# Attention and mixture layers in one pipelined kernel: other order and other buffers in the first and in the last iterations

## What is computed

```python
x = x + attn_a(layernorm(x))     # 16 heads of 8 channels, rotary, causal
x = x + ffn(layernorm(x))
x = x + attn_b(layernorm(x))     # the same form, other weights and angles
x = x + ffn(layernorm(x))

def ffn(x):                      # 8 heads of 64 channels, 5 experts, 2 picked
    wv = topk_mask(x @ Ws, 2) * sigmoid(x @ Ws)          # per token and head
    v = einsum('bthe,btek->bhtk', wv, einsum('btd,edk->btek', x, Wv))
    probs = softmax(einsum('bhid,bhjd->bhij', q * scale, k))
    attn = einsum('bhij,bhjd->bihd', probs, v)
    return einsum('bthe,bthk,ekd->btd', topk_mask(x @ Wd, 2), attn, Wo)
```

## Time and profile before

| | value |
|---|---|
| median of 3 runs | 1955.2 us |
| the profiled execution's own time | 1959.13 us |
| its span, first to last instruction | 1957.4 us |
| PE busy | 1787.4 us (91%) |
| DVE busy | 1570.6 us (80%) |
| ACT busy | 1274.1 us (65%) |
| POOL busy | 1049.5 us (54%) |
| mean granted TensorE clock | 0.977 |
| PE in the 40 slices of the span | 4878999999999999999999999999999999998894 |

### The profile page before, as it was taken

How to read it: one execution, slowest core, us unless ns; L and a number is a source line. 1 busy time by engine, 2 the same in 40 slices (tenths; PEclk the granted TensorE clock), 3 DMA queues, 4 the chain that set the end, 5 groups by cost and what they waited for, 6 DMA issues and landing times.

```text
span 1957.4 us, 32660 instructions
## 1 busy us (share of the span) xinstructions
PE 1787.4 (91%) x11328; PEld 894.7 (46%) x11328; DVE 1570.6 (80%) x2936; ACT 1274.1 (65%) x2803; POOL 1049.5 (54%) x1124
## 2 busy tenths in 40 slices
PE   4878999999999999999999999999999999998894
PEld 2343545445454544545455454544545454453443
DVE  6487888889888798988879788887978888797661
ACT  1547577675857768586775857667585766758461
POOL 1416374665637466463746646374664647555533
PEclk8989999999999999999999999999999999999887
DMA  2211011110101111110111111011110101100000
GB/s 78 62 43 33 12 39 39 45 39 31 47 12 40 38 45 39 31 44 15 39 39 45 38 31 36 22 39 39 44 40 31 31 28 39 39 11 21 1 11 6
DMA packets 87361, 66.61 MB, mean 34 GB/s; under 512 B 10592, under 2 KB 82976, under 8 KB 87200
## 3 DMA queue, kind: packets, MB, share of 16 engines
q1 hardware_dynamic: 87200, 64.52, 10.8%
HBM read 30.42 MB, written 8.39 MB: 20 GB/s over the span
## 4 chain that ended last, share of the span: by engine, by line
PE 54%; DVE 30%; ACT 10%; issue 3%; POOL 1%; DMA 1%; SPq 0%; POOLq 0%; PEld 0%; DVEq 0%; PEldq 0%; ACTq 0%
PE Y L494 9%; DVE nmaxA L877 7%; DVE ztmp L992 6%; PE S1c L433 5%; PE S2a L459 4%; PE S1b L433 4%; DVE nmaxF L882 4%; ACT Pq L721 4%; PE S2b L459 4%; PE Y L485 4%; PE M L587 3%; PE M L545 3%; ACT PT L706 3%; DVE ztmp L964 2%; PE M L599 2%
## 5 line engine op out<-in xcount | busy, mean ns | idle before, releaser
L1110 POOL TENSOR_TENSOR Z<-Z,ztmp 128x1280 f32<-128x1280 f32 x112 | 324.6, 2898 | 339.9 <-DVE ztmp L992 338.8
L1077 POOL TENSOR_SCALAR_AFFINE_SELECT PT<-PT 128x256 f32<-128x256 f32 (+1 forms) x640 | 256.3, 410 | 290.9 <-ACT PT L706 285.8
L1101 POOL TENSOR_TENSOR Vf<-Vf,ztmp 128x512 f32<-128x512 f32 x256 | 349.0, 1363 | 94.4 <-DVE ztmp L964 85.8
L706 ACT ACTIVATE PT<-S2a 128x512 f32<-128x512 f32 x320 | 191.8, 599 | 132.5 <-PE S2a L453 126.1
L494 PE MATMUL Y<-PT,Vf 128*64 128x512 f32 x1024 | 267.8, 614 | 0.0
L710 ACT ACTIVATE PT<-S2a 128x512 f32<-128x512 f32 x256 | 153.4, 599 | 151.5 <-PE S2a L459 148.1
L964 DVE TENSOR_TENSOR ztmp<-xv,wv_s 128x512 f32<-128x512 f32 x256 | 240.2, 938 | 2.8 <-POOL Z L1110 2.8
L433 PE MATMUL S1c<-Kf,Qf 64*128 64x512 f32 x352 | 201.8, 654 | 26.8 <-ACT Pq L721 25.7
L433 PE MATMUL S1a<-Kf,Qf 64*128 64x512 f32 x352 | 201.4, 652 | 25.6 <-ACT Pq L721 25.6
L706 ACT ACTIVATE PT<-S2b 128x512 f32<-128x512 f32 x320 | 191.9, 600 | 25.9 <-PE S2b L453 25.6
L433 PE MATMUL S1b<-Kf,Qf 64*128 64x512 f32 x320 | 183.3, 653 | 10.2 <-ACT Pq L721 10.1
(11 more groups left out here) (111 smaller groups left out, 3729.8 us busy)
## 6 DMA issues: line engine op xcount, KB each, us to landing
Qs<-parts SPq DMA_DIRECT2D x96, 128.0 KB
Ks<-parts SPq DMA_DIRECT2D x96, 128.0 KB
tab_s<-in_tab SPq DMA_DIRECT2D x16, 512.0 KB, 4.4
out_x<-res SPq DMA_DIRECT2D x32, 256.0 KB, 2.2
xr<-out_x SPq DMA_DIRECT2D x24, 256.0 KB, 2.9
wa_s<-in_wa SPq DMA_DIRECT2D x16, 320.0 KB, 3.2
xl<-in_x SPq DMA_DIRECT2D x8, 256.0 KB, 3.0
Qs<-mrowA SPq DMA_DIRECT2D x128, 4.0 KB, 1.7
```

The costliest lines, as they stand in the source:

```text
L706: nc.scalar.activation(PT[:, slot % 2, b, :], t[:, :], ACT.Exp, scale=SCALE_A).then_inc(exps_done.sem, 1)
L1101: nc.gpsimd.tensor_tensor(Vf[:, i, :, :], Vf[:, i, :, :], vtmp[:, n % VBUF, :, :], ALU.add).then_inc(v_acc.sem, 1)
L1110: nc.gpsimd.tensor_tensor(Z[:, :, :, :], Z[:, :, :, :], ztmp[:, hh % 2, :, :, :], ALU.add).then_inc(z_acc.sem, 1)
```

## The change

It touches iterations 0, 17 and 18; the code of the others is as before.

- Iteration 0: the keys are rotated in `first_keys`, memory of `Pq` that has no use yet, so their rotation waits no longer for the queries' third part. The 6 scatters of the keys are issued by ACT. All 98 rows of `Ks` are set to ones in one memset of 4-byte words; the memset of two rows is gone. PE steps over absent uses with fewer waits.
- Iteration 17: the order of uses is `LAST_USES`, with "F q2" and "F k2" ahead of "YT7", and their projection is at (0, 6), not (1, 6). The product of the last head (hh = 7) is at (2, 5), not (1, 3). The buffers of the value products lie in `PT`, and the second value product waits no longer for the last sum into Z. Uses that have no work are all stepped over at the iteration's start.
- Iteration 18: heads 4 and 5 are multiplied as before, but POOL adds only tokens 256 to 511 (the second half of the four 128-token tiles), and DVE the first half. Heads 6 and 7 are multiplied and added by DVE alone, half by half. Transposes, copies, the product with `wo_s`, the residual and the store come in two halves, in the banks S1a to S1c, S2a and S2b.

```diff
...
+    TWO_ONES = float(np.array([0x3F803F80], np.uint32).view(np.float32)[0])
...
+        first_keys = Pq[:, 0, 0:2, :]
...
+        LAST_USES = ["YT6", "F q2", "F k2", "YT7", "F q3", "F k3", "ZT0", "ZT1", "ZT2", "F out", "YT4", "YT5"]
...
-                late = [u for u in uses if u in ("ZT0", "ZT1", "ZT2", "F out")]
-                uses = [u for u in uses if u not in late]
-                first = uses.index("A yNT" if "A yNT" in uses else "YT2")
-                uses = uses[:first] + late + uses[first:]
+                uses = [u for u in uses if u not in LAST_USES] + [u for u in LAST_USES if u in uses]
...
+        def f_steps(k):
+            return F_STEPS[:2] + [(0, 6)] + F_STEPS[3:] if k == UNITS + 1 else F_STEPS
+        def mix_step(k, g, h):
+            return (2, 5) if (k, g, h) == (UNITS + 1, 3, 1) else ((SA + g + 2) % NS, 2 * h + 1)
+        def vtmp_of(k, n):
+            return PT[:, n % VBUF // 2, NF_B + n % 2, :].rearrange("p (h d) -> p h d", h=HF) if k == UNITS + 1 else vtmp[:, n % VBUF, :, :]
...
+        def turning(j, qk):
+            return (first_keys[:, 0, :], first_keys[:, 1, :]) if j == 0 and qk else (rot, rot2)
...
-                if f_end:
+                if f_end and j < LAST - 1:
                     sp.wait_ge(resF_ready.sem, resF_ready.at(j, 1, 3))
                     sp.dma_start(stream(j - 3), res[:, :, :]).then_inc(resF_stored.sem, 16)
+                if j == LAST - 1:
+                    for half in range(2):
+                        sp.wait_ge(tail_ready, half + 1)
+                        sp.dma_start(stream(j - 3)[:, HALVES[half], :], res[:, HALVES[half], :]).then_inc(tail_stored, 16)
...
+                        if j == 0 and qk:
+                            continue
...
+                    if j == UNITS + 1 and use not in LAST_USES and not at_start:
+                        return
+                    if j or place(j, use) > place(j, "A xnT" if use in M0_USES else "A q"):
+                        pe.wait_ge(*free_for(j, use))
                     pe.sem_inc(is_full(use), 1)
                     pe.sem_inc(is_free(use), 1)
...
+                def last_output():
+                    for half in range(2):
+                        pe.wait_ge(tail_sums, half + 1)
+                        for c, (lo, hi) in enumerate(ZCH):
+                            for i in range(NT)[HALVES[half]]:
+                                zi = Z_wide[:, i, :, :].rearrange("p e d -> p (e d)")
+                                last = nc.tensor.transpose(S1[c][0:hi - lo, i * P:(i + 1) * P], zi[:, lo:hi], ident[:, :])
+                            last.then_inc(tail_ZT_filled, 1)
+                        pe.wait_ge(tail_ZT_drained, len(ZCH) * (half + 1))
+                        for i in range(NT)[HALVES[half]]:
+                            for c, (lo, hi) in enumerate(ZCH):
+                                last = nc.tensor.matmul(S2[half][:, i * C:(i + 1) * C], ZT[0:hi - lo, c, i * P:(i + 1) * P],
+                                                        wo_s[0:hi - lo, c, :], start=(c == 0), stop=(c == 2))
+                        last.then_inc(tail_out_filled, 1)
...
+                at_start = True
+                if j == UNITS + 1:
+                    for use in M0_USES + M1_USES:
+                        if use not in LAST_USES:
+                            skip(use)
+                at_start = False
...
+                        if j == LAST - 1 and at == (1, 0):
+                            last_output()
...
-                        if at in F_STEPS:
-                            f_project(F_STEPS.index(at))
+                        if at in f_steps(j):
+                            f_project(f_steps(j).index(at))
...
+                        if j == 0 and at == (4, 4):
+                            act.wait_ge(rows_zeroed.sem, rows_zeroed.per)
+                            act.wait_ge(part2_ready.sem, part2_ready.at(j, 2))
+                            for r in range(NSP):
+                                act.dma_start(Ks[rows_of(r), :, :],
+                                              parts[:, 1, SPLITS_K[r], :]).then_inc(scattered.sem, 16)
...
+                        if j == LAST - 1 and at == (1, 1):
+                            for half in range(2):
+                                for c, (lo, hi) in enumerate(ZCH):
+                                    act.wait_ge(tail_ZT_filled, len(ZCH) * half + c + 1)
+                                    nc.scalar.activation(ZT[0:hi - lo, c, tokens(half)], S1[c][0:hi - lo, tokens(half)],
+                                                         ACT.Copy).then_inc(tail_ZT_drained, 1)
...
+                    rot, rot2 = turning(j, qk)
+                    if qk and half == 0 and j:
...
-                    if i == 0 and e == 1:
+                    if i == 0 and e == 1 and j <= UNITS:
                         dve.wait_ge(z_acc.sem, z_acc.at(j, HF - 1, 3))
                     n = i * (E - 1) + e
                     if e and n > VBUF:
                         dve.wait_ge(v_acc.sem, v_acc.at(j, n - VBUF, 2))
                     nc.vector.tensor_tensor(
-                        vtmp[:, n % VBUF, :, :] if e else Vf[:, i, :, :],
+                        vtmp_of(j, n) if e else Vf[:, i, :, :],
...
+                def last_product(hh, half):
+                    g, h = divmod(hh, GF)
+                    own = HALVES[half]
+                    y = bank(f"YT{SA + g}")[:, :].rearrange("p (t h d) -> p t h d", t=NT, h=GF)
+                    nc.vector.tensor_tensor(
+                        ztmp[:, h, own, :, :], y[:, own, h:h + 1, :].broadcast_to([P, NT // 2, E, DF]),
+                        wz[:, :, own, hh].rearrange("p e t -> p t e").unsqueeze(3).broadcast_to([P, NT // 2, E, DF]),
+                        ALU.mult).then_inc(tail_mixed, 1)
+                def last_sum(hh, half, done):
+                    own = HALVES[half]
+                    nc.vector.tensor_tensor(Z[:, own, :, :], Z[:, own, :, :], ztmp[:, hh % 2, own, :, :],
+                                            ALU.add).then_inc(done, 1)
+                def last_sums_in_front():
+                    dve.wait_ge(z_acc.sem, z_acc.at(j, 3, 3))
+                    dve.wait_ge(z_mult.sem, z_mult.at(j, 5, 3))
+                    last_sum(4, 0, tail_mixed)
+                    dve.wait_ge(z_mult.sem, z_mult.at(j, 6, 3))
+                    dve.wait_ge(tail_mixed, 1)
+                    last_sum(5, 0, tail_mixed)
+                def last_pair():
+                    dve.wait_ge(*filled(j, f"YT{NS - 1}"))
+                    dve.wait_ge(tail_mixed, 2)
+                    last_product(6, 0)
+                    last_product(7, 0)
+                    dve.wait_ge(tail_mixed, 3)
+                    last_sum(6, 0, tail_mixed)
+                    dve.wait_ge(tail_mixed, 5)
+                    last_sum(7, 0, tail_sums)
+                    dve.wait_ge(z_acc.sem, z_acc.at(j, 5, 3))
+                    last_product(6, 1)
+                    last_product(7, 1)
+                    dve.wait_ge(tail_mixed, 6)
+                    last_sum(6, 1, tail_mixed)
+                    dve.wait_ge(tail_mixed, 8)
+                    last_sum(7, 1, tail_sums)
+                    dve.sem_inc(is_free(f"YT{NS - 1}"), 1)
+                def last_output():
+                    dve.wait_ge(xrF_loaded.sem, xrF_loaded.at(j, 1, 3))
+                    dve.wait_ge(resA_stored.sem, resA_stored.at(j, 1, 2))
+                    for half in range(2):
+                        dve.wait_ge(tail_out_filled, half + 1)
+                        nc.vector.tensor_tensor(res[:, HALVES[half], :].rearrange("p t c -> p (t c)"), S2[half][:, tokens(half)],
+                                                xr[:, HALVES[half], :].rearrange("p t c -> p (t c)"), ALU.add).then_inc(tail_ready, 1)
...
-                        for rows in (Qs, Ks):
-                            nc.vector.memset(rows[0:ROWS_P1, :, :], 0.0).then_inc(rows_zeroed.sem, 1)
-                    if j == 0 and slot == SA:
-                        nc.vector.memset(Ks[ROWS_P1:ROWS_P2, :, :], 1.0).then_inc(ones_ready.sem, 1)
+                        nc.vector.memset(Qs[0:ROWS_P1, :, :], 0.0).then_inc(rows_zeroed.sem, 1)
+                        nc.vector.memset(Ks[:, :, :].rearrange("p h t -> p (h t)").bitcast(F32),
+                                         TWO_ONES).then_inc(rows_zeroed.sem, 1)
...
-                        if b in (1, 3) and slot in (0, 1, 6, 7) and (f if slot > 1 else f_end):
-                            if (slot, b) == (6, 1):
-                                f_mix_weights()
-                            f_mix((slot - 2) % NS - SA, b // 2, 3 if slot < 2 else 2)
+                        if at == (6, 1) and f:
+                            f_mix_weights()
+                        for g, h in ((g, h) for g in range(SF) for h in range(GF)):
+                            if at == mix_step(j, g, h) and (f if g < 2 else f_end) and (j < LAST - 1 or g == 2):
```

(8 more changed lines are left out.)

54 lines of the change are left out of this document (32 added, 22 removed).

## The result

| kernel | median | runs | against before, 95% interval |
|---|---|---|---|
| before | 1955.11 us | 7 | |
| the change | 1960.84 us | 7 | 1.0033 [1.0021, 1.0044] |

The change is **slower**: by 5.7 us between the medians, and by 4.1 to 8.6 us by the interval of the ratio. That is only 0.3%, but clear of the noise. I had forecast 1950.3 us, faster than before, with a range to 1954.0, so the forecast missed in sign. The profiled execution of the change took 1960.84 us, which is its median; that of before took 1959.13 us, 4.0 above its own. So the two traces differ by only 1.7 us, and the other 4.0 lie in something that the trace of before doesn't show as it usually is.

The account below looks back on a forecast made before the run. The chain ran through PE for 54% and DVE for 30%; only start, iteration 17 and tail counted. -1.5 + 0.7 - 4.1 = -4.9 took the profiled 1959.13 to 1954.2, less 3.9 for the median: 1950.3 us, range 1945.0 to 1954.0.

Parts of the forecast that it names:

- 'YT6' is drained at 1838.9 (1835.99 + 2.89): Iteration 17: YT6 drained at 1838.9, then PE projects at once, making YT7 2.3 us later than before.
- the median shown is 3.9 below it, so 1950.3: Whole kernel: the forecast profiled execution of 1954.2 us is lowered by 3.9 to give the median.
- Rival 1: Iteration 17: scores run at the high clock, gaining 3.9 us in place of losing 0.7, so 1945.7; chance 0.12.
- a second projection 0.7 later: Iteration 17: projection at 1869.0 in place of 1868.35, the first maximum's head start of 5.0 us being eaten.
- rival 2: Iteration 17: POOL gets its turn between the two first products, ending 2.1 us later than before, 1951.7; chance 0.17.
- The walk behind it: Iteration 17: waits followed from the first maximum through the three-bank score loop to the second projection, 0.7 us later.
- Rival 4: Iteration 17: every value product waits a full sum; 8.3 us lost, 1957.9; decides if second projection starts after 1873.9; chance 0.05.
- Start: Iteration 0: keys ready at 27.7 and first scores at 34.9, 1.5 us earlier, since their rotation waits less.
- Rival 3: Iteration 0: the start gives nothing, ACT issuing more slowly or both scatters sharing engines; 1951.8 us; chance 0.13.
- Tail: Iteration 18: work in halves lets the last store be issued 4.1 us earlier; ends 3.0 and 4.8.
- the good end: Tail: half of the last six output products runs at the high clock level, making the gain 4.8 us.
- what follows the store, 12.6, stays: Tail: the time from the last store's issue to the span's end stays at 12.6 us.

Follow-up runs that it names:

- e1: The change, but PE steps over iteration 17's 25 absent uses with a few counted waits and increments instead of one by one; ratio to before 0.9989.
- e10: The kernel before with six more semaphores, each raised once at the program's end; executed once, 117.9 us from iteration 17's YT6 transposes to the end.
- e3: The change with iteration 17 written as in the kernel before, keeping the new start and tail; ratio to before 0.9974.
- e4: e3 with the keys' turning and scattering at the start also as before, leaving mainly the tail in halves; ratio to before 0.9979.
- e11: e7 with head 7's product moved to step (2, 2), behind the third maximum; ratio to before 0.9978.
- e2: The change, but absent uses stepped over one by one at their old places and head 7's product at its old step; ratio to before 0.9992.
- e7: e8 with iteration 17's value products and their sums moved behind the first four maxima; ratio to before 0.9987.
- e8: e1 with head 7's product back at its old step, ahead of the first maxima; ratio to before 0.9997.
- e16: e3 with iteration 17's value products and sums moved behind the first four maxima; ratio to before 0.9998.
- e14: e15 with the late value products and sums of e16 added; ratio to before 0.9993.
- e15: e3 with eight extra matmuls of 128x512 filling PE's pause ahead of iteration 17's first projection; ratio to before 0.9987.
- e12: The same kernel as e3, run once more as a repeat; ratio to before 0.9987.

## Why the prediction was wrong

**The step that failed.** "'YT6' is drained at 1838.9 (1835.99 + 2.89)" took YT6's time over from the trace of before. Nothing in the sum stands for the 25 steps that the change puts at the iteration's start; they were costed at nothing, as if a step were no work. 25 uses, two increments of 0.15 us each, stand in PE's queue right ahead of the transposes on which ACT, DVE and POOL all wait. They cost 5.4 us at the transposes (1839.01 in place of 1833.6), 6.6 at the second projection, since PE came out of the pause at the low clock, and 5.7 over the whole stretch (the change against e1). The price could be read: in the chain of waits of the kernel before, the two increments of the same `skip`, 0.15 us apart, stand on the path at the very end:

```profile
1938.46 0.05 PEldq L391
1938.51 0.10 issue
1938.61 0.06 PEldq L392
1938.67 0.19 issue
```

The Trainium skill (TensorE: Matmul & The Clock Gate, section "The cost: per-tile semaphore tail") gives about 26 ns for each increment that hangs on a matmul. No run here shows that one; the increment as an instruction of its own, which this kernel uses, takes 150 ns in the rows above, and by these it has to be priced.

**The second step that failed** is the base: "the median shown is 3.9 below it, so 1950.3". An offset between one execution and the median was carried over as if it belonged to every version. The change's profiled execution has no such offset. In the profiled execution of before the scores ran at 0.50; in e10's, 1954.14 us, at 1.00, and the difference, 4.2 us in the stretch, is about that offset. The record has the mean granted clock of 140 more executions of the kernel before: the 25 with 0.976 to 0.978 took 1956.7 to 1959.6 us, and the other 115 took 1954.4 in the median. So the profiled one (0.977, 1959.13) is of the rarer kind for the kernel before, while six of the seven executions of the change had 0.975 to 0.978. Rival 1's price (3.9 + 0.7) was near, then, but it held for the kernel before and not for the change: the clock fell early in the scores in all traces of its order without added matmuls. The mean clock of an execution doesn't say in which stretch it was low, so that the median of before stands for runs with the scores at 1.00 is argued and not shown.

**Iteration 17 besides.** The forecast was a second projection 0.7 later with DVE winning its turns; rival 2 said 2.1 with POOL between the two first products. The rows have rival 2's order: POOL's sum started at 1849.87, ahead of the product at 1850.30, which then took 3.37 us. In e1, free of the steps, the first maximum came 2.3 us earlier than before (13.4 against 15.6 us behind YT6), where rival 2 said 2.0 and the forecast 5.0. The walk behind it overstated the loss: the second projection is 1.2 later than before (34.15 against 32.98), between the two. Behind that point the forecast put nothing ("From there PE is the bound in both"), but e1 loses about as much again to e3 there, mostly at the low clock. That the stretch of e1 against e3 gives rival 2's 2.1 to the tenth is therefore chance. The moved projection did run in 1.98 us, as forecast.

**Rival 4** named the right mark, a second projection later than 1873.9, and it came at 1874.38; but its mechanism (a turn for every value product) is not in the rows, where most of them take 0.68 to 0.77. The steps at the start brought it there.

**Start:** 1.5 forecast, 1.25 in the change, 1.3 in e3 against e4. The keys were ready at 27.6, as said (27.7); ACT issues six scatters in 4.49 us, slower than SP's 3.87, and the first scores followed 7.6 us later in place of 7.2. Rival 3 (no gain at the start) didn't come.

**Tail:** 4.1 forecast, 4.3 measured by e4 (5.0 in the trace of the change). That they are so near is luck, two errors against each other. Up to the first half's products all is within 0.4 us (1932.60 against 1932.95 on the clock of before). The second half ran at the full clock in that trace: its transposes in 0.8 us where I had 1.55, its products in 1.60 where I had 2.5 (the good end had half of that). So the last store came 2.1 us earlier than forecast. But "what follows the store, 12.6, stays" was wrong: 13.85.

Summed on the profiled execution: -1.3 + 5.7 + 2.1 - 4.3 = +2.2, 1961.3; measured 1960.84. The last three are differences along a row of traces (before, e4, e3, e1, the change), so up to rounding they must come to the difference of the stretches, 3.4; what the sum tests is that little else changed ahead of them. The 4.0 that are missing against the median of before are most likely the clock that it has and the change has lost.

What came out ahead of both kernels: the change's two ends with the old iteration 17 (e3: 0.9974 and 0.9987), the tail alone (0.9979), and the moved projection with counted steps, late sums and late values (e11: 0.9978). These three are not told apart.

## What to carry to other kernels

Bookkeeping on an engine's queue is work: count the waits and increments that a reordering puts ahead of an instruction others wait for, price them from the chain of waits, and fold a run of them into one counted increment (e1), or leave them where the engine waits anyway (e2). Before a sum is set against one profiled execution, see whether that execution is the usual one; where the clock differs within a stretch, each version may have its own usual level. And where DVE and POOL take turns, moving an operation pays if it gets out of the way of a sum (e7 against e8), and costs if no sum was there (e16 against e3, e14 against e15).

## What the runs showed of the hardware

An increment as an instruction of PE's queue takes 0.15 us, and a wait that is already fulfilled adds little to it (6.1 us for the 41 increments from 1832.01 to 1838.12; with or without a wait between two of them they stand 0.15 apart, rarely 0.19). Six DMA issues on ACT took 4.49 us against 4.06 and 3.87 on SP. Between DVE's products of two SBUF inputs and POOL's sums, the one that started first went first in the rows shown here: a sum that began 0.43 us ahead held the product for 2.7 us (3.37 in place of 0.68). TensorE's granted clock from 1850 to 1863 us of the same program was 0.56 in one execution and 1.00 in another (e3 and e12), with PE busy 13.00 and 12.18 of 13 us in it.
